# Dense experts that add up in four PSUM banks under the token's share, and second-attention projections from high and low parts

## What is computed

```
hmid = jax.nn.gelu(x @ w1e + b1e, approximate=False)
return (acc + (hmid @ w2e + b2e) * ce[:, None], None)
```

```
qkv = x @ W_attn.T + b_attn
q, k, v = jnp.split(qkv, 3, axis=-1)
```

## Time and profile before

| | before |
|---|---|
| median of 3 runs | 1095.7 us |
| the profiled execution, its own time | 1094.63 us |
| its span | 1092.9 us |
| busy, share of the span | PE 87%, DVE 71%, ACT 59%, POOL 45% |
| granted TensorE clock, mean | 0.93 |

### The profile page before, as it was taken

The page is one execution under the profiler, slowest core; times in us unless marked ns, Lnnn a source line. Parts: engine busy times, 40 slices in busy tenths (PEclk is TensorE's granted clock), DMA queues, the critical chain, the costliest instruction groups (busy, mean ns, idle before and its releaser), DMA issues. The chain is left out here.

```text
span 1092.9 us, 20105 instructions
## 1 busy us (share of the span) xinstructions
PE 955.5 (87%) x6024; PEld 605.4 (55%) x6024; DVE 773.3 (71%) x2421; ACT 639.5 (59%) x1418; POOL 488.2 (45%) x590
## 2 busy tenths in 40 slices
PE   2999999985999999987999899999999998960696
PEld 1444444433788888873445565556555655650585
DVE  4567677725898989887889888879887987443121
ACT  1366565642777777763566657665767566730253
POOL 4132332212122222211466867686668668924155
PEclk9999999955899999997999999999999988975798
DMA  3000000004400000000000000000000000005730
GB/s 89 1 2 1 1 1 1 2 1 152 110 29 20 19 19 19 10 1 1 1 1 1 1 2 1 1 2 1 2 1 2 1 1 1 1 1 191 230 119 14
DMA packets 23415, 28.80 MB, mean 26 GB/s; under 512 B 3340, under 2 KB 19729, under 8 KB 23328
## 3 DMA queue, kind: packets, MB, share of 16 engines
q1 hardware_dynamic: 21168, 24.53, 7.3%
q0 software_dynamic: 1728, 3.17, 0.8%
q10 hardware_dynamic: 432, 0.01, 0.0%
HBM read 20.57 MB, written 8.04 MB: 26 GB/s over the span
## 5 line engine op out<-in xcount | busy, mean ns | idle before, releaser
L1114 POOL TENSOR_SCALAR probs<-probs,rinv 128x128 f32<-128x128 f32 (+3 forms) x256 | 274.4, 1087 | 122.6 <-DVE rinv L990 122.6
L1058 ACT ACTIVATE pt<-psum 128x128 f32<-128x128 f32 (+3 forms) x256 | 98.4, 434 | 110.3 <-PE psum L863 109.1
L1049 ACT ACTIVATE probs<-probs,rowmin 128x128 f32<-128x128 f32 (+3 forms) x256 | 141.4, 558 | 32.6 <-DVE rowmin L984 31.3
L984 DVE CUSTOM_DVE_ANT_0 probs<-psum,adj 128x128 f32<-128x128 f32 (+3 forms) x256 | 122.1, 477 | 43.1 <-PE psum L853 26.4
L535 ACT ACTIVATE pT<-psum 128x1024 f32<-128x1024 f32 (+3 forms) x128 | 89.9, 702 | 69.0 <-PE psum L365 67.4
L853 PE MATMUL psum<-k_sb,q_sb 64*128 64x256 f32 (+3 forms) x512 | 113.2, 495 | 16.7 <-DVE rowmin L984 16.2
L474 DVE TENSOR_REDUCE top<-psum 128x2 f32<-128x256 f32 (+3 forms) x128 | 101.7, 817 | 24.8 <-PE psum L353 24.6
L973 DVE MAX8 top<-w 128x8 f32<-128x131 f32 (+3 forms) x208 | 103.2, 496 | 4.6
L1458 ACT ACTIVATE m_hid<-psum,b1t 128x512 f32<-128x512 f32 x128 | 88.2, 689 | 24.2 <-DVE m_hid_lo L1332 21.9
L863 PEld LDWEIGHTS psum<-ident,probs 128*128 128x128 f32 x640 | 68.7, 142 | 59.6 <-POOL probs L1114 32.2
L863 PE MATMUL psum<-ident,probs 128*128 128x128 f32 x640 | 100.1, 288 | 0.7 <-POOL probs L1114 0.7
(11 more groups left out here) (242 smaller groups left out, 1941.9 us busy)
## 6 DMA issues: line engine op xcount, KB each, us to landing
s_wb<-in_w_all SPq DMA_DIRECT2D x15, 514.5 KB
sorted_x<-blank SPq DMA_DIRECT2D x1, 3870.0 KB, 19.8
s_xg<-sorted_x SPq DMA_DIRECT2D x15, 258.0 KB, 5.6
m_w1s<-in_w SPq DMA_DIRECT2D x16, 128.0 KB, 2.1
m_w2s<-in_w SPq DMA_DIRECT2D x16, 128.0 KB, 2.1
x_tok<-in_x SPq DMA_DIRECT2D x4, 256.0 KB, 4.0
bv<-in_b_v SPq DMA_DIRECT2D x1, 512.0 KB, 4.9
wq<-in_wq SPq DMA_DIRECT2D x1, 512.0 KB, 4.5
```

Source lines behind the costliest of these rows:

```text
L984: dve.tensor_tensor_reduce(probs[:, k, 0:K], s_bank[h][:, 0:K], adj[:, OFF[i]:OFF[i] + K], 1.0, FLOOR, ALU.add, ALU.min, rowmin[:, k:k + 1 ...
L1049: act.activation(probs[:, k, 0:K], probs[:, k, 0:K], ACT.Exp, bias=rowmin[:, k:k + 1], scale=-1.0, accum_out=rsum[:, k:k + 1]).then_inc(ex ...
L1058: act.activation(pt[:, (2 * n + h) % 4, 0:K], t_bank[h][:, 0:K], ACT.Copy).then_inc(pt_ready, 1)
L1114: pool.tensor_scalar(probs[:, k, 0:K], probs[:, k, 0:K], rinv[:, k:k + 1], None, ALU.mult).then_inc(normed, 1)
```

## The change

In the dense experts the share now multiplies the gelu's result, before the second product: `dve_scale` takes a unit's 128x1024 hidden values times `share`, the shares of 512 tokens, the same in every partition. ACT then rounds the scaled values to `hid_hi` in one 128x1024 copy (`act_round`), DVE makes `hid_lo` in one 128x1024 instruction, and the second product adds into `o_bank[k]`, one bank per chunk for all 16 experts. ACT's copy, the transposes and the addition to `x_tok` happen once per chunk, after the last expert; the bias b2 comes in by one matmul per chunk. The router works chunk by chunk inside the norm's loop; the shares of a chunk are turned by PE, copied by ACT, stored to DRAM by SP and loaded back into all partitions, for two experts ahead.

In the second attention q, k and v come from three fp32r matmuls each, of high and low parts. DVE makes the low part of the tokens (`dve_split_x`), once per sequence. The weights are loaded in the first attention and split there by POOL in 12 pieces of 256 columns (a cast and a subtraction each).

```
+                    pool.tensor_copy(hi_c, raw_c).then_inc(w1_high, 1)
+                    pool.wait_ge(w1_high, n + 1)
+                    pool.tensor_tensor(lo_c, raw_c, hi_c.bitcast(F32), ALU.subtract).then_inc(w1_split, 1)
...
+                        if r % 4 == 2 and r >= 8 and r // 4 - 2 < SPLITS:
+                            pool_split(pool, r // 4 - 2)
...
-                        pe.wait_ge(f_act, act_no["x", b, 0])
-                        mm = pe.matmul(bank[:], wq[:, j, :], xb[:], start=True, stop=True)
+                        pe.wait_ge(x_split, b + 1)
+                        pe.matmul(bank[:], wq1_hi[:, j, :], xb_hi[:], start=True, stop=False)
+                        pe.matmul(bank[:], wq1_lo[:, j, :], xb_hi[:], start=False, stop=False)
+                        mm = pe.matmul(bank[:], wq1_hi[:, j, :], xb_lo[:], start=False, stop=True)
...
+                def dve_split_x(dve, use):
+                    dve.wait_ge(f_act, act_no[use])
+                    dve.tensor_tensor(xb_lo[:], fill_bank(use)[:], xb_hi[:].bitcast(F32),
+                                      ALU.subtract).then_inc(x_split, 1)
...
+                    dve_split_x(dve, FIRST[0])
...
                 def pe_second(pe, e, u, k):
 
+                    first, last = isinstance(e, int) and e == 0, isinstance(e, int) and e == E - 1
+                    pe.wait_ge(lo_ready, LEAD + e * CH + k + 1)
                     for f in range(NF):
+                        pe.matmul(o_bank[k][:], w2_hi[:, u, f, :], hid_hi[:, k % HB, f, :], start=first and f == 0,
+                                  stop=False, skip_group_check=True)
+                        pe.matmul(o_bank[k][:], w2_lo[:, u, f, :], hid_hi[:, k % HB, f, :], start=False, stop=False,
+                                  skip_group_check=True)
+                        mm = pe.matmul(o_bank[k][:], w2_hi[:, u, f, :], hid_lo[:, k % HB, f, :], start=False,
+                                       stop=last and f == NF - 1, skip_group_check=True)
                     mm.then_inc(expert_out, 1)
...
+                    pe.matmul(o_bank[k][:], b2_e[:], comb_e[:, k, :], start=False, stop=False, skip_group_check=True)
...
-                            if k or u or not isinstance(t, int) or t:
-                                pe_back(pe, *before(e, k))
-                    if last:
-                        pe_back(pe, e, CH - 1)
+                            if isinstance(t, int) and t == 0 and u == 1:
+                                pe_bias(pe, k)
...
+                    for q in range(CH):
+                        pe.wait_ge(comb_ready, q + 1)
+                        pe.transpose(o_bank[q][0:E * TC, 0:P], comb[:, q, :, :].rearrange("p e t -> p (e t)"),
+                                     ident[:]).then_inc(comb_turned, 1)
...
+                def dve_scale(dve, e, u, k, t):
+                    n = e * CH + k
+                    if k == 0:
+                        dve.wait_ge(share_in[u], 16 * CH + 16 * t)
+                    dve.wait_ge(hid_full, LEAD + (n + 1) * NF)
+                    h = hid[:, k % HB, :, :]
+                    dve.tensor_tensor(h, h, share[:, u, k, :].unsqueeze(1).to_broadcast([P, NF, 512]),
+                                      ALU.mult).then_inc(scaled, 1)
...
+                    dve.wait_ge(rounded, n + 1)
+                    dve.tensor_tensor(hid_lo[:, k % HB, :, :], hid[:, k % HB, :, :],
+                                      hid_hi[:, k % HB, :, :].bitcast(F32), ALU.subtract).then_inc(lo_ready, 1)
...
+                            if k + 1 < CH or u == 0 or not last:
+                                dve_low(dve, *later(e, u, k, 1))
                             if k + LOOK < CH or u == 0 or not last:
-                                dve_low(dve, *later(e, u, k))
-                            if k or u or not isinstance(t, int) or t:
-                                dve_acc(dve, *before(e, k))
-                    if last:
-                        dve_acc(dve, e, CH - 1)
+                                e2, u2, k2 = later(e, u, k, LOOK)
+                                dve_scale(dve, e2, u2, k2, t if u == 0 or k + LOOK < CH else t + 1)
...
-                        if q >= 2:
+                        if 2 <= q <= CH + 1:
                             dve_split(dve, q - 2)
+                            dve_logits(dve, step, q - 2)
+                        if q >= 3:
+                            dve_route(dve, step, q - 3)
...
+                    dve_scale(dve, 0, 0, 0, 0)
+                    dve_low(dve, 0, 0, 0)
+                    dve_scale(dve, 0, 0, 1, 0)
...
+                        act.activation(hid[:, k % HB, f, :], h_bank[(k * NF + f) % 4][:], ACT.Gelu,
+                                       bias=b1t0[:, bass.ds(e * NF + f, 1)]).then_inc(hid_full, 1)
+
+                def act_round(act, e, u, k):
                     n = e * CH + k
+                    act.wait_ge(scaled, n + 1)
+                    act.wait_ge(expert_out, LEAD + n + 1 - HB)
                     apart(act, passed)
+                    act.activation(hid_hi[:, k % HB, :, :], hid[:, k % HB, :, :], ACT.Copy).then_inc(rounded, 1)
...
+                            if k + 1 < CH or u == 0 or not last:
+                                act_round(act, *later(e, u, k, 1))
                             if k + LOOK < CH or u == 0 or not last:
-                                act_hidden(act, *later(e, u, k))
-                            act_out(act, e, k)
+                                act_hidden(act, *later(e, u, k, LOOK))
...
+                    act_hidden(act, 0, 0, 0)
+                    act_comb(act, 0)
+                    act_comb(act, 1)
+                    act_hidden(act, 0, 0, 1)
+                    act_comb(act, 2)
+                    act_comb(act, 3)
+                    act_round(act, 0, 0, 0)
...
+                    for q in range(CH):
+                        sp.wait_ge(comb_copied, q + 1)
+                        sp.dma_start(shares[q].rearrange("e (t p) -> (e t) p", p=P), comb_t[:, q, :]).then_inc(comb_stored, 16)
+                        sp.wait_ge(comb_stored, 16 * (q + 1))
+                        for u in range(2):
+                            sp.dma_start(share[:, u, q, :], shares[q, u].partition_broadcast(P)).then_inc(share_in[u], 16)
...
+                            sp.wait_ge(scaled, (t * 2 + u + 1) * CH)
+                            sp.dma_start(share[:, u, :, :], shares[:, e, :].rearrange("q e n -> (q e) n").partition_broadcast(P)).then_inc(share_in[u], 16)
```

More of the change, by code:

```diff
@@ L1036, in act_drain @@
                     if kind == "x":
-                        ins = act.activation(xb[:], bank[:], ACT.Copy)
+                        ins = act.activation(xb_hi[:], bank[:], ACT.Copy)
                     elif kind == "q":
@@ L1222, in experts0, with later @@
                 y_back = s_("y_back")
-                acc = s_("acc")
                 h_bank = banks[0:4]
-                o_bank = banks[4:6]
-                back_bank = banks[6:8]
-                def act_rounds(f):
-                    return f % 2 == 0
-                ROUND_D = sum(not act_rounds(f) for f in range(NF))
+                o_bank = banks[4:8]
+                def later(e, u, k, by):
+                    return (e, u, k + by) if k + by < CH else (e + 1, 1 - u, k + by - CH)
                 def pe_first(pe, e, u, k):
@@ L1390, in dve_split, with dve_logits @@
                                       ALU.subtract).then_inc(xt_split, 1)
+                def dve_logits(dve, c, q):
+                    ts = slice(q * TC, (q + 1) * TC)
+                    lp = o_bank[q][:, 0:TC * E].rearrange("p (t e) -> p t e", e=E)
+                    dve.wait_ge(logits, q + 1)
+                    c.count(dve.tensor_tensor(lg[:, ts, :], lp, rb0[:].unsqueeze(1).to_broadcast([P, TC, E]),
+                                              ALU.add).then_inc(router_step, 1))
+                    c.count(dve.memset(pr[:, ts, E:RW], 2.0).then_inc(router_step, 1))
+                    dve.wait_ge(router_step, c.done())
+                    c.count(dve.tensor_reduce(mx[:, ts], lg[:, ts, :], AX.X, ALU.max).then_inc(router_step, 1))
+                    dve.wait_ge(router_step, c.done())
+                    dve.tensor_tensor(lg[:, ts, :], lg[:, ts, :], mx[:, ts].unsqueeze(2).to_broadcast([P, TC, E]),
+                                      ALU.subtract).then_inc(shifted, 1)
@@ L1392, in dve_program @@
                 def dve_program(dve):
-                    lead(dve, (lo_ready, acc))
+                    lead(dve, (lo_ready,))
                     c = Steps(0, 2 * T + CH)
-                    for q in range(CH + 2):
+                    step = Steps(0, CH * (10 + 2 * TC))
+                    for q in range(CH + 3):
                         if q < CH:
@@ L1412, in dve_program @@
-                    step.count(dve.memset(pr[:, :, E:RW], 2.0).then_inc(router_step, 1))
-                    dve.wait_ge(router_step, step.done())
```

(19 more changed lines are left out.)

282 lines of the change are left out of this document (146 added, 136 removed).

## The result

The changed kernel took **1160.7 us** in the median of four runs (1157.5 to 1162.6), the kernel before 1095.2 in its own four (1094.2 to 1095.9): ratio **1.060, 95% interval 1.057 to 1.063**, slower. The forecast was 1152, its range 1116 to 1182. The profiled execution took 1162.6 us, with a span of 1160.8; the one of before took 1094.6, so 67.9 us have to be found. All medians here are of fast executions; one of e6's four runs was slow, at 1699.3 us, and is left out of its median.

What follows compares the result with a forecast made beforehand. PE bounded the dense units before; the change makes an ACT-DVE ring the bound. Units +46, ahead of them +18, end -1, second attention -9, first attention +2: +56 on 1094.6, 1150.6, stated as 1152 us, range 1116 to 1182.

Steps and rivals of the forecast that it cites:

- The circle: Dense units: ACT and DVE alternate, each waiting for the other; a unit takes 3.68 us written out, 3.85 in the loop.
- +46: Dense units: 3.83 and 4.00 us a unit against 3.23, together 46 us more; bounds +20 to +67.
- the signs named: Dense units, if right: PE busy about 75%, PE waiting for m_hid_lo, rounding for m_hid, roundings 3.8 to 4.0 us apart.
- POOL's share of DVE: Dense units: POOL's weight splitting delays DVE's instructions, taken as 0.15 us a unit.
- rival 3: Dense units: POOL's four pieces each hold DVE in full, 25 us more, 1177 us; chance 0.08.
- The forecast's upper end: Dense units: POOL's four pieces each held against DVE in full, 2.2 us per expert, 0.55 a unit.
- Ahead of the units: Routing by chunk and shares through memory: first second product at 303 us, 18 us later; bounds +12 to +24.
- The clearing of `sorted_x`: Dense experts: blanking moved behind the share loads ends before the third expert's weights are due, costing nothing.
- The second attention: Shorter projections save 12 us of 15 off PE, late splits cost 2 and 1: -9 us (-16 to +3).
- rival 4: Dense units: PE's idling lowers the clock; half of the units at half clock add 38 us, 1190 us; chance 0.05.
- Rival 1: Dense units: PE stays the bound through two units of lookahead, 2.8 us a unit, 1079 us; chance 0.04.
- Rival 2: Dense units: 1024-wide DVE instructions run at twice the pace, 0.7 us each, ring 3.3, 1110 us; chance 0.05.

Runs made afterwards that it cites:

- e6: The change with ACT's and DVE's lists both turned, scaling in two halves, and the clearing of sorted_x behind the loop: 1126.2 us, ratio 1.029.
- e1: The change with both lists turned (ACT: gelus before rounding; DVE: scaling before subtraction): 1135.6 us, ratio 1.039.
- e2: The change with ACT's list alone turned (gelus before rounding), DVE's left: 1160.7 us, ratio 1.062.
- e4: The change with POOL splitting only one column of the weights of experts 2 to 15: 1149.5 us.
- e3: The change with each chunk's shares transposed and copied earlier, and the first expert's share loads issued before the second's: 1156.3 us.
- e5: The change with e3's share chain, and the clearing of sorted_x issued after the loop over the experts: 1152.0 us.
- e7: The kernel before with only the change's second attention, its dense-expert bias b2 loaded in a wrong layout: 1091.3 us, ratio 0.997.
- e9: e8 with scaling whole again, first products three units ahead instead of two, and POOL splitting w1 earlier: 1088.8 us, ratio 0.994.
- e10: e7 with the bias loaded as before and the low part of x made ahead of twelve tiles of statistics: 1092.1 us, ratio 0.998.
- e8: e6 with e3's share chain, and in the second attention the low part of x made ahead of twelve tiles of statistics: 1118.2 us, ratio 1.021.

## Why the prediction was right or wrong, point by point

**The circle was right**, and the runs show it by its two ends: turning both lists takes 25 us off with the same work (e1), turning one takes nothing (e2). Its sum, 3.68 written out, measured 3.62 undisturbed: the handoff from ACT to DVE was 0.03 where I had 0.12, every other term came within 0.02. The 1.22 for the scaling (measured 1.23) does not follow from the numbers given with it, as 0.69 plus 512 elements at the pace of 1.21 for 1024 make 1.30; the step from a 768- to a 1024-wide reduction (0.95 to 1.21 us) does give it. In the loop I had 0.17 more, taking 0.32 us for the handoff from DVE to ACT out of the earlier trace rows; it measured 0.14 there too (411.95 to 412.09). That 0.32 was a wait for PE's last matmul, another kind of releaser. So "+46" was really (3.79 - 3.23) x 63 = 35, with 3 more around it. Of the signs named, the rounding's wait for `m_hid` came true, and its distance of 3.79 us in the mean is at the lower edge of the 3.8 to 4.0 named; PE was busy 81%, not 75%.

**POOL's share of DVE**, put at 0.15 us a unit, measured 0.17 (e4), and rival 3 fell. The rows above show how it comes about, and most other experts repeat them. DVE's subtraction starts at 405.15, 0.04 behind POOL's at 405.11, and takes 0.56 longer than undisturbed; the scaling starts at 406.86, inside POOL's cast of 406.02, and takes 0.18 longer. POOL's own last two pieces start inside DVE's instructions and take 1.17 and 1.60 in place of 0.40 and 0.74. The Trainium skill, SBUF — State Buffer, "SBUF: two separate sides", has the port pair as an exclusive lock that whoever starts first keeps for the whole instruction. The rows agree with it as far as they go: each engine is held by what the other had begun. The forecast's upper end had all four pieces hold DVE in full; here the first met DVE idle, two cost it 0.56 and 0.18, and the last waited itself: 0.74 us an expert in place of 2.2. No run takes the lock itself apart.

**Ahead of the units** "+18" was +29. The shares were ready at 296.4, near the 293.5 forecast. What failed is "Then one after another: transpose, ACT's copy and handoffs 1 us; store 2.1 and load 2.3": I followed the last chunk alone, as if the earlier three had gone. They were queued ahead of it, at 4.2 us each, and started late by ACT's and PE's order. e3 and e5 show it: the same work and transfers in another order begin the units 9.8 us sooner. That is nearly all of the 11 us missed; the shares themselves were ready 36.8 us after the first statistics where I had 35.2.

**The clearing of `sorted_x`**, put at nothing, was nothing in the change, as the units came late and slowly. e3 shows how thin that cover was: 10 us sooner, and it took back 6.

**The second attention** "-9" was -3.2. The failed step is "where less PE work gives nothing: I take 12". The saving of a projection held: its start to the next scores took 0.95 in the earlier trace rows and 0.88 for one of x and wq now,

```profile
775.92 0.48 PE L845 MATMUL psum<-xb_hi,wq_hi 128*128 128x512 f32 x1
776.24 0.39 PE L846 MATMUL psum<-xb_hi,wq_lo 128*128 128x512 f32 x1
776.47 0.40 PE L847 MATMUL psum<-xb_lo,wq_hi 128*128 128x512 f32 x1
776.80 0.92 PE L893 MATMUL psum<-k_sb,q_sb 64*128 64x384 f32 x4
```

but most took 1.06 before (709.82 to 710.88), so the 0.95 was a low one and the 0.79 forecast for the new one too; the difference is the 0.16 forecast. PE's busy time falls by 3.8 us for the 24 projections of a sequence, 0.16 each. But the gain came in the second and third sequence, 3.0 us each, in the change and in every later run with this attention. The first sequence, before and after:

```profile
517.00:637.70 120.70, 114.49 (x714) 63.63 (x712) 103.08 (x375) 77.64 (x220) 77.28 (x79) 0.99 0.00 1
```

```profile
589.70:710.30 120.60, 110.68 (x747) 70.32 (x745) 103.80 (x377) 77.44 (x221) 77.14 (x79) 0.98 0.00 1
```

PE has 3.8 us less to do and the stretch is as long. PE's waits for DVE, busy 104 of 121 us there, took most of it up: they went from 6.2 to 9.3 us, those for the row minimum among them from 4.0 to 5.5.

In the second sequence DVE has more room:

```profile
637.70:748.90 111.20, 108.43 (x760) 63.50 (x758) 92.35 (x343) 74.75 (x217) 80.31 (x81) 1.00 0.01 1
```

```profile
710.30:818.40 108.10, 104.61 (x782) 68.00 (x782) 92.51 (x342) 74.53 (x218) 80.20 (x81) 1.00 0.01 1
```

and the same 3.8 us show as 3.1. At the start of the block the first exponential came 3.8 us later (30.4 against 26.6 after the block began), where I had +2. PE waited for the low part of x until 567.64, 8.4 us into the block (5.3 before), which is what I had forecast (498.6 less 490.4). The larger part is the clock. From 9.6 to 20.6 us into the block it was granted at 1.00 before, 0.50 in the change and 0.76 in e2:

```profile
500.00:511.00 11.00, 10.29 (x30) 4.39 (x30) 8.54 (x35) 4.97 (x8) 0.40 (x4) 1.00 0.00 1
```

```profile
568.90:579.90 11.00, 10.07 (x21) 5.83 (x21) 4.79 (x17) 2.17 (x4) 0.39 (x4) 0.50 0.00 0
```

```profile
569.90:580.90 11.00, 9.84 (x29) 5.79 (x28) 6.58 (x26) 3.79 (x6) 0.39 (x4) 0.76 0.01 1
```

e2 and e3 have the same code there and the same wait until 8.4 us, and their first exponential came at 27.4 and 27.6 us. So the late split is worth about 1 us, and 3 us of the 3.8 belong to the clock of that execution; why it came back later than before no run tells. The sum, 3.8 - 3.0 - 3.0 and -1 in the last sequence, is the -3.2 of this pair of traces; in e2 and e3 the block is 5.9 and 5.8 us shorter than before, in e1 as long. Over 12 runs e7 has -3.9 for the whole kernel. The gain on PE was thus 7 us where I took 12.

**The clock** was granted at 0.99 in the units with PE idle a fifth of the time, so rival 4 fell. Rival 1, PE as the bound at 2.8 us a unit, is what e9 measured, with lists that allow it; "the lookahead fills PSUM, not the scaled values" named what was missing. Rival 2 fell by the 1.23 us of the scaling.

**Left out of the forecast altogether:** the four products that add the bias (below). In the change, PE's waits covered most of it. The sparse experts' +2.3 us is work that the change does not touch. The profiles put it to the clock as well, which came back 4 us later; from 54 to 64 us into the block, before and after:

```profile
1019.70:1029.70 10.00, 8.78 (x32) 6.73 (x33) 1.27 (x3) 3.46 (x9) 0.00 (x0) 0.71 1.04 334
```

```profile
1085.30:1095.30 10.00, 8.62 (x21) 6.23 (x22) 0.85 (x2) 2.52 (x6) 0.00 (x0) 0.50 1.07 350
```

It is so in all runs with the new dense experts, but also in e10 with the old ones, and not in e7; so the new dense experts are not needed for it, and the cause stays open.

**The total** owes something to luck. Against the profiled execution the forecast was 12 us low: units 6 too many, start 11 too few, second attention 6 too few, sparse experts 2 too few. The first two errors have different causes, and had they not partly cancelled, it would have been 18. The first attention's +1.3 against +2 tells nothing, as it varies by more than that between executions.

## What to carry to other kernels

When work is moved from one engine to two others that hand it to each other, follow each engine's list in order and look for a circle: if an instruction waits for the answer to the one just ahead of it on its own queue, buffers don't help, and the period is the sum of the steps, however idle each engine is. Cut it by placing between the two an instruction of another unit, on both engines. Then look for the next, longer circle and give it distance: here the third unit of lookahead, with the weights split earlier, took 29 us more off. With the order of a few transfers all of it was worth 72 us of 1161. A small difference in a block that was not touched is compared with the same block in other executions, and with the clock granted there, before it gets a cause. A chain through memory is priced with all that is queued ahead of its last piece, and each large transfer that nobody waits for goes behind those that someone does.

## What was not expected of the hardware

Four intervals among the units 5 to 10 are long in e1, e6, e8 and e9, in e9 at 4.03 to 4.12 us though PE is never idle. The cause is in PE's timeline (of e9): behind the second products of expert 1 the bias is added by a plain fp32 product with 16 rows,

```profile
324.27 0.40 PE L1316 MATMUL psum<-m_hid_lo,m_w_hi 128*128 128x512 f32 x1
324.60 1.12 PE L1324 MATMUL psum<-m_comb_e,m_b_e 16*128 16x512 f32 x2
325.65 0.50 PE L1301 MATMUL psum<-m_xt_hi,m_w_hi 128*128 128x512 f32 x1
```

and the next first product starts 1.38 us after the last of the unit, where 0.23 is usual: with a unit of 4.04 in place of 2.77, 4 x 1.3 = 5 us for a term that has an eighth of the rows. From 324.60 to 325.65 this product takes 1.05 us, as an fp32 projection with all 128 rows did before (1.06, at 709.82): fewer rows saved nothing. And one transfer of 3.9 MB held the issue of the next behind it on SyncE's queue for 12.9 us (e3; 9.9 in the change), not only its landing, so that all that SyncE was to issue later stood too. In e5, with that transfer behind the loop, the same issue took 1.0 us.
